# A perceiver kernel: the latents' own keys handled as one full 128-row tile, high and low part in one

## The reference

```
xn = _layernorm(x, ln1_w, ln1_b)            # the context, 1024 rows a batch
ln = _layernorm(latents, ln2_w, ln2_b)      # the 64 latents
q = ln @ Wq
kv = concatenate([xn, ln], axis=-2) @ Wkv   # 1024 context keys, then 64 own keys
k, v = split(kv, 2)                         # 16 heads of 64
logits = einsum('bhld,bhsd->bhls', q * scale, k * scale)
out = einsum('bhls,bhsd->bhld', softmax(logits), v)
return out.reshape(B, L, INNER) @ Wo
```

## Time and profile before

| | us |
|---|---|
| median of 3 runs (lowest, highest) | 920.51 (920.04, 922.19) |
| the profiled execution | 921.28 |
| its span, first to last instruction | 919.6 |
| PE busy | 812.8 |
| DVE busy | 530.1 |
| ACT busy | 385.0 |
| POOL busy | 256.7 |

### The profile page before, as it was taken

The page is one execution under the profiler, slowest core; times in us unless marked ns, Lnnn a source line. Parts: engine busy times, 40 slices in busy tenths (PEclk is TensorE's granted clock), DMA queues, the critical chain, the costliest instruction groups (busy, mean ns, idle before and its releaser), DMA issues.

```text
span 919.6 us, 13716 instructions
## 1 busy us (share of the span) xinstructions
PE 812.8 (88%) x5443; PEld 699.2 (76%) x5443; DVE 530.1 (58%) x992; ACT 385.0 (42%) x888; POOL 256.7 (28%) x179
## 2 busy tenths in 40 slices
PE   5899999999999999999999999997636565788996
PEld 3589999999999999999999999984312232257885
DVE  5364565555555555556547453445899999971112
ACT  2444444443544443444444343432853434403341
POOL 3717008008005205303502600001245545610000
PEclk9999999999999999999999999997858989898998
DMA  8100100100100010010030100000200000061720
GB/s 297 46 1 1 47 1 2 46 2 1 42 6 1 6 42 1 1 47 1 2 115 1 10 1 1 1 1 2 92 0 0 0 1 0 0 240 37 273 92 25
DMA packets 22499, 34.21 MB, mean 37 GB/s; under 512 B 6488, under 2 KB 18336, under 8 KB 21408
## 3 DMA queue, kind: packets, MB, share of 16 engines
q1 hardware_dynamic: 22432, 33.29, 10.6%
HBM read 32.77 MB, written 0.52 MB: 36 GB/s over the span
## 4 chain that ended last, share of the span: by engine, by line
PE 76%; DVE 16%; issue 4%; DMA 1%; ACT 1%; SPq 0%; DVEq 0%; POOL 0%; POOLq 0%; ACTq 0%
PE psum L1155 21%; PE psum L1193 20%; DVE state L782 12%; PE psum L1176 6%; PE psum L1197 4%; PE psum L1128 3%; PE psum L1475 3%; PE psum L1465 3%; PE psum L1216 2%; PE psum L1111 2%; PE psum L1135 2%; PE psum L1226 2%; PE psum L1207 2%; PE psum L1288 1%; DMA wq_sb<-in_L_xattn_Wq_dram 1%
## 5 line engine op out<-in xcount | busy, mean ns | idle before, releaser
L901 ACT ACTIVATE pt_hi<-psum 128x512 fp32r<-128x512 f32 (+1 forms) x192 | 87.0, 488 | 268.6 <-PE psum L1176 169.8
L624 DVE TENSOR_TENSOR pt_lo<-psum,pt_hi 128x512 fp32r<-128x512 f32 (+1 forms) x192 | 100.3, 550 | 101.4 <-ACT pt_hi L901 101.2
L1193 PE MATMUL psum<-kvn_hi,pt_hi 128*128 128x256 f32 x512 | 149.6, 292 | 0.0
L1193 PE MATMUL psum<-kvn_lo,pt_hi 128*128 128x256 f32 x512 | 144.0, 281 | 0.0
L1193 PE MATMUL psum<-kvn_hi,pt_lo 128*128 128x256 f32 x512 | 143.8, 281 | 0.0
L632 DVE TENSOR_REDUCE rowmax<-psum 128x1 f32<-128x728 f32 x64 | 58.7, 918 | 110.0 <-PE psum L1155 110.0
L782 DVE TENSOR_TENSOR_SCAN state<-dec,drive 128x2048 f32<-128x2048 f32 x16 | 107.1, 6691 | 0.1
L1193 PEld LDWEIGHTS psum<-kvn_lo,pt_hi 128*128 128x128 f32 x512 | 97.3, 190 | 0.1
L1193 PEld LDWEIGHTS psum<-kvn_hi,pt_hi 128*128 128x128 f32 x512 | 97.1, 190 | 0.1
L1193 PEld LDWEIGHTS psum<-kvn_hi,pt_lo 128*128 128x128 f32 x512 | 97.1, 190 | 0.0
L1155 PE MATMUL psum<-kvt_hi,qk_hi 128*128 128x364 f32 (+1 forms) x384 | 90.7, 345 | 4.3 <-ACT prob L939 2.5
(11 more groups left out here) (216 smaller groups left out, 1471.0 us busy)
## 6 DMA issues: line engine op xcount, KB each, us to landing
w<-in_L_ffn_W_dram SPq DMA_DIRECT2D x16, 1024.0 KB, 7.5
ctx_nat<-in_ctx_dram SPq DMA_DIRECT2D x8, 1024.0 KB, 4.9
wk_nat<-in_L_xattn_Wkv_dram SPq DMA_DIRECT2D x1, 1024.0 KB, 6.5
wq_sb<-in_L_xattn_Wq_dram SPq DMA_DIRECT2D x1, 1024.0 KB, 11.7
wv<-in_L_xattn_Wkv_dram SPq DMA_DIRECT2D x1, 1024.0 KB, 13.9
wo<-in_L_xattn_Wo_dram SPq DMA_DIRECT2D x1, 1024.0 KB, 16.2
q_t<-in_L_attn_W_in_dram SPq DMA_DIRECT2D x1, 1024.0 KB, 7.4
x_lat<-in_x_dram SPq DMA_DIRECT2D x1, 512.0 KB, 3.7
```

The source lines that it names most:

```text
L624: dve.tensor_tensor(pt_lo[u][rows, t0:t1, :], where[rows, 0:(t1 - t0) * P].rearrange("p (t m) -> p t m", m=P), pt_hi[u][rows, t0:t1, :].bi ...
L901: act.activation(pt_hi[u][rows, t0:t1, :], where[rows, 0:(t1 - t0) * P].rearrange("p (t m) -> p t m", m=P), ACT.Copy)\
L1193: pe.matmul(PV, w[u][:, j, :], x_[slot][:, j, :], start=(j == 0 and w is pt_hi and x_ is kvn_hi), stop=False)
```

## The change

The own keys are treated as a full tile of 128 rows. A third Exp writes the 64 own probabilities a second time behind the first (`prob` becomes 64 columns wider). One transpose of these 128 columns then gives the turned own probabilities twice, on the upper and the lower 64 partitions. ACT evacuates both into `pt_hi`; DVE then replaces the half `half(1)` (partitions 64 to 127) by the low part, value minus its high part. The latents are laid out on both halves as well: SP copies them by two DMAs inside the SBUF from `x_lat` to the two halves of `lat_cur`, and POOL makes `cur_hi` on all 128 partitions and `cur_lo` on the first 64, the rest staying zero. `cur_hi` and `cur_lo` have a buffer for each slot. The product with `cur_hi` then gives hi x hi + lo x hi in one matmul, the one with `cur_lo` hi x lo. The turn is the same in even and odd blocks.

```diff
@@ -77,8 +77,8 @@
         qk_lo = [sb(att, f"qk_lo{i}", [P, CK, HP, 2, L], F32R) for i in range(2)]
         x_lat = sb(att, "x_lat", [P, TT, C])
         lat_cur = sb(att, "lat_cur", [P, C])
-        cur_hi = sb(att, "cur_hi", [P, C], F32R)
-        cur_lo = sb(att, "cur_lo", [P, C], F32R)
+        cur_hi = [sb(att, f"cur_hi{i}", [P, C], F32R) for i in range(2)]
+        cur_lo = [sb(att, f"cur_lo{i}", [P, C], F32R) for i in range(2)]
         latt_hi = sb(att, "latt_hi", [P, CK, T], F32R)
         latt_lo = sb(att, "latt_lo", [P, CK, T], F32R)
 
@@ -86,7 +86,7 @@
         wk_t = sb(att, "wk_t", [P, HP, C])
         wv = sb(att, "wv", [P, CK, INNER])
         wo = sb(att, "wo", [P, HP, C])
-        prob = [sb(att, f"prob{i}", [P, S + L]) for i in range(2)]
+        prob = [sb(att, f"prob{i}", [P, S + 2 * L]) for i in range(2)]
         y_n = sb(att, "y_n", [P, C])
         y_t = sb(att, "y_t", [P, CK, P])
         o_t = sb(att, "o_t", [P, HP, P])
@@ -119,7 +119,7 @@
         kvn_hi[1] = sb(att, "kvn_hi1", [P, SJ, C], F32R)
         kvn_lo[1] = sb(att, "kvn_lo1", [P, SJ, C], F32R)
         pt_hi = [sb(att, f"pt_hi{i}", [P, SJ + 1, P], F32R) for i in range(2)]
-        pt_lo = [sb(att, f"pt_lo{i}", [P, SJ + 1, P], F32R) for i in range(2)]
+        pt_lo = [sb(att, f"pt_lo{i}", [P, SJ, P], F32R) for i in range(2)]
         att.close()
 
 
@@ -238,6 +238,7 @@
         TWO = psum[:, 0:2, :]
         CUT = 364
         LG_A, LG_B = psum[:, 0:2, 0:CUT], psum[:, 2, 0:S + L - 2 * CUT]
+        LG_OWN = psum[:, 2, S - 2 * CUT:S + L - 2 * CUT]
         TP, PV, OC, MB = [psum[:, 3, :], psum[:, 4, :]], psum[:, 5, 0:C], psum[:, 6, :], psum[:, 7, :]
 
         XB = (0, 1, 3, 6)
@@ -247,6 +248,7 @@
         ld_xlat, ld_vec, ld_wq, ld_wk, ld_wvo, ld_ctx = (sem(n) for n in (
             "ld_xlat", "ld_vec", "ld_wq", "ld_wk", "ld_wvo", "ld_ctx"))
         ld_vec2 = sem("ld_vec2")
+        ld_lat = sem("ld_lat")
         ld_mam, ld_idx, ld_comb, ld_b2, ld_out = (sem(n) for n in ("ld_mam", "ld_idx", "ld_comb", "ld_b2", "ld_out"))
         ld_e = [sem(f"ld_e{i}") for i in range(RING)]
 
@@ -351,11 +353,19 @@
             sp.dma_start(wo[:], Wo.rearrange("(h p) n -> p h n", p=P)).then_inc(ld_wvo, 16)
             sp.dma_start(x1[:], x.rearrange("(t b) l c -> (b l) t c", b=BP)).then_inc(ld_wvo, 16)
 
+            def load_latents(b):
+                for h in range(2):
+                    sp.dma_start(lat_cur[half(h)], x_lat[half(b % BP), b // BP, :]).then_inc(ld_lat, 16)
+
+            sp.wait_ge(s_pln, 1)
+            load_latents(0)
             for b in range(1, B):
                 sp.wait_ge(s_misc, MISC * b)
                 sp.wait_ge(s_klo, b)
                 sp.dma_start(ctx_nat[:], ctx_in[b].rearrange("(p j) c -> p j c", j=SJ))\
                     .then_inc(ld_ctx, 16)
+                sp.wait_ge(s_lcur, 2 * b)
+                load_latents(b)
 
             sp.wait_ge(s_qcur, 2 * B)
             sp.dma_start(win[:], W_in.rearrange("(k p) n -> p k n", p=P)).then_inc(ld_mam, 16)
@@ -421,6 +431,8 @@
 
             link(pool.memset(ident[:], 0.0))
             link(pool.memset(q_cur[:], 0.0))
+            for slot in range(2):
+                link(pool.memset(cur_lo[slot][half(1)].bitcast(F32), 0.0))
             pool.affine_select(out=ident[:], in_=ident[:], compare_op=ALU.not_equal, fill=1.0, base=0,
                                pattern=[[-1, P]], channel_multiplier=1).then_inc(s_id, 1)
             link(pool.memset(mhalf[:], -0.5))
@@ -436,7 +448,7 @@
 
                 pool.wait_ge(s_misc, MISC * (b - 1) + 4)
                 apart(pool)
-                pool.wait_ge(s_lcur, 3 * b)
+                pool.wait_ge(s_lcur, 2 * b)
                 apart(pool)
                 for h in range(2):
                     rows = slice(h * DH, (h + 1) * DH)
@@ -445,17 +457,14 @@
 
             def latents(b, slot):
 
-                rows = half(slot)
-                flat = x_lat[:].rearrange("p t c -> p (t c)")
+                top_rows = half(0)
                 pool.wait_ge(s_klo, b + 1)
                 apart(pool)
-                pool.tensor_copy(lat_cur[rows], flat[rows, ds((b - slot) * (C // BP), C)]).then_inc(s_lcur, 1)
-                pool.wait_ge(s_lcur, 3 * b + 1)
-                apart(pool)
-                pool.tensor_scalar(cur_hi[rows], lat_cur[rows], 1.0, 0.0, ALU.mult, ALU.add).then_inc(s_lcur, 1)
-                pool.wait_ge(s_lcur, 3 * b + 2)
-                pool.tensor_tensor(cur_lo[rows], lat_cur[rows], cur_hi[rows].bitcast(F32), ALU.subtract)\
-                    .then_inc(s_lcur, 1)
+                pool.wait_ge(ld_lat, 32 * (b + 1))
+                pool.tensor_scalar(cur_hi[slot][:], lat_cur[:], 1.0, 0.0, ALU.mult, ALU.add).then_inc(s_lcur, 1)
+                pool.wait_ge(s_lcur, 2 * b + 1)
+                pool.tensor_tensor(cur_lo[slot][top_rows], lat_cur[top_rows], cur_hi[slot][top_rows].bitcast(F32),
+                                   ALU.subtract).then_inc(s_lcur, 1)
 
             def context(b, slot):
 
@@ -498,7 +507,7 @@
                     queries(b + 1)
                     context(b + 1, 1 - slot)
                     latents(b + 1, 1 - slot)
-                    pool.wait_ge(s_lcur, 3 * (b + 2))
+                    pool.wait_ge(s_lcur, 2 * (b + 2))
 
             all_steps(body, lambda b, slot, pair: None)
 
@@ -620,10 +629,12 @@
                 high, low, where, t0, t1 = {"A": (s_hA, s_lA, TP[0], 0, 4), "B": (s_hB, s_lB, TP[1], 4, 8),
                                             "C": (s_hC, s_lC, TP[0], 8, 9)}[part]
                 dve.wait_ge(high, count(b, hp))
-                rows = slice(0, P) if part != "C" else half(slot)
-                dve.tensor_tensor(pt_lo[u][rows, t0:t1, :],
-                                  where[rows, 0:(t1 - t0) * P].rearrange("p (t m) -> p t m", m=P),
-                                  pt_hi[u][rows, t0:t1, :].bitcast(F32), ALU.subtract).then_inc(low, 1)
+                if part == "C":
+                    dve.tensor_tensor(pt_hi[u][half(1), SJ, :], where[half(1), 0:P],
+                                      pt_hi[u][half(1), SJ, :].bitcast(F32), ALU.subtract).then_inc(low, 1)
+                    return
+                dve.tensor_tensor(pt_lo[u][:, t0:t1, :], where.rearrange("p (t m) -> p t m", m=P),
+                                  pt_hi[u][:, t0:t1, :].bitcast(F32), ALU.subtract).then_inc(low, 1)
 
             def step(b, slot, hp, live, more, pair):
                 p1, p3 = back(b, slot, hp, 1), back(b, slot, hp, 3)
@@ -897,9 +908,8 @@
                 turned, high, where, t0, t1 = {"A": (s_tA, s_hA, TP[0], 0, 4), "B": (s_tB, s_hB, TP[1], 4, 8),
                                                "C": (s_tC, s_hC, TP[0], 8, 9)}[part]
                 act.wait_ge(turned, count(b, hp))
-                rows = slice(0, P) if part != "C" else half(slot)
-                act.activation(pt_hi[u][rows, t0:t1, :],
-                               where[rows, 0:(t1 - t0) * P].rearrange("p (t m) -> p t m", m=P), ACT.Copy)\
+                act.activation(pt_hi[u][:, t0:t1, :],
+                               where[:, 0:(t1 - t0) * P].rearrange("p (t m) -> p t m", m=P), ACT.Copy)\
                     .then_inc(high, 1)
 
             def mean_value(now):
@@ -936,8 +946,10 @@
                     act.activation(prob[hp % 2][:, 0:2 * CUT].rearrange("p (a n) -> p a n", n=CUT), LG_A, ACT.Exp,
                                    bias=nbias[slot][:, hp:hp + 1], scale=SCALE,
                                    accum_out=den_part[slot][:, hp, 0:1])
-                    act.activation(prob[hp % 2][:, 2 * CUT:], LG_B, ACT.Exp, bias=nbias[slot][:, hp:hp + 1],
-                                   scale=SCALE, accum_out=den_part[slot][:, hp, 1:2]).then_inc(s_exp, 1)
+                    act.activation(prob[hp % 2][:, 2 * CUT:S + L], LG_B, ACT.Exp, bias=nbias[slot][:, hp:hp + 1],
+                                   scale=SCALE, accum_out=den_part[slot][:, hp, 1:2])
+                    act.activation(prob[hp % 2][:, S + L:], LG_OWN, ACT.Exp, bias=nbias[slot][:, hp:hp + 1],
+                                   scale=SCALE).then_inc(s_exp, 1)
                 if more and hp == MISC - 1:
                     misc_hi(b + 1, 1 - slot, hp)
                     own_rows(b + 1, 1 - slot)
@@ -1161,11 +1173,7 @@
                 if part == "C":
                     pe.wait_ge(s_lA, count(b, hp))
                     apart(pe)
-                    if slot == 0:
-                        last = pe.transpose(TP[0][0:L, 0:P], prob[hp % 2][:, S:S + L], ident[:])
-                    else:
-                        last = pe.matmul(TP[0][half(slot), 0:P], prob[hp % 2][:, S:S + L], ident[:],
-                                         start=True, stop=True)
+                    last = pe.transpose(TP[0][:, 0:P], prob[hp % 2][:, S:S + 2 * L], ident[:])
                     last.then_inc(s_tC, 1)
                     return
                 before = back(b, slot, hp, 1)
@@ -1183,7 +1191,7 @@
```

(7 more changed lines are left out.)

## The result

| | before | after |
|---|---|---|
| median, us | 920.35 | 892.92 |
| lowest to highest | 920.04 to 922.19 | 892.84 to 893.45 |
| the profiled execution (span) | 921.28 (919.6) | 892.84 (891.1) |
| first logits to the end of the stage's last L1226 / L1233 | 39.58 to 627.90: 588.3 | 39.09 to 601.87: 562.8 |
| behind the attention stage | 291.7 | 289.3 |

The ratio is 0.9699, with a 95% interval of 0.9682 to 0.9716: 27.4 us faster. The forecast was 894.5.

A forecast was written before the change was run, and what follows sets the result against it. TensorE was taken as the bound. Gains of 25.7 us in steps and 0.7 in the drain, less 0.2 for the Exp, gave 26.2 off 921.28, stated as 894.5 us for the median; range 890 to 904.

The forecast's parts named there:

- The bound and the way to read it: Attention stage: TensorE has no idle time to fill, so only giving it less work gains; costs read from ends.
- Parts 1 and 2: Own products and turn: one product (0.12) and shape changes into (0.19) and out of 64 rows (0.13) go; turn 0.11.
- Part 3: Head's output behind a full-width transpose at step end: 0.38 us, taken as already carrying a shape entry.
- The first rival: At the head's output the shape change is only moved: step gains 0.22 to 0.30, about 904 us; chance 0.14.
- The sum: Attention stage: 25.7 us from the steps plus 0.7 in the drain, 26.4; less 0.2 for the Exp, 26.2.
- Part 4: ScalarE's third Exp: signal 0.12 to 0.23 later, hidden behind TensorE, cover left 0.3 to 0.4; 0.2 charged at start.
- two covers at the ends of steps: Last step of a block: 0.95 us before the next block's logits, and over 2 us for the Exp itself.
- Parts 6 and 7: GpSimd loses one copy (0.39) and SP gains two on-chip copies per block, both under cover: nothing charged.

The follow-up runs named there:

- the run with equal work: Changed kernel with its second own product (cur_lo) on the upper 64 rows only, as many matmuls as before that edit: 914.25 us.
- two-product variant: Kernel before the change with its third own product (low probabilities times high latents) left out, two 64-row products staying: 911.89 us.

## Why the prediction was right

- *The bound and the way to read it.* Right: before the change TensorE had no idle time from the third step to the drain, and less work for it went into the time almost one for one.
- *Parts 1 and 2, product, two changes of shape, turn.* Right in each term. The product is 0.12 by the run without it (a step of 8.53 against 8.65) and about 0.10 by the run with one more (6.5 us in the stage); the shape is 0.34 at its place and 0.32 in the mean of all steps by the run with equal work, against 0.32 from the earlier trace rows.
- *Part 3, 0.38 for the head's output behind a full turn.* Right: 0.38 in both parities and in the drain. I had taken it from the earlier trace rows, the one place where L1216 stood behind a certain change. The first rival (902 to 907) fails. L1216 took 0.38 behind L1165, though both are shown 128*64, and the trace of the kernel before has a border there. Behind the transpose L1165 the loads for L1216 start 0.23 later, together with their matmul:

```profile
234.54 0.11 PEld L1165 LDWEIGHTS psum<-ident,prob 128*64 128x64 f32 x1
234.77 0.31 PEld L1216 LDWEIGHTS psum<-y_t,wv 128*64 128x64 f32 x8
```

  Behind L1167 of odd blocks, a plain matmul in the same shape, L1216 starts 0.01 later. This is explained if L1165 worked as a full-array instruction. It fits what the Trainium skill says in "TensorEngine Tiling (Array Packing)", "Restrictions", on transposes and column tiling; no run separates it from another cause. The drain that the Trainium skill names in the same page's "Key Properties" agrees with the loads that start late at every border looked at here.
- *The sum.* Forecast 26.2 in the attention stage, measured 25.5. Odd blocks gave 0.40 to 0.43 a step but for hp = 3. Even blocks gave 12.4 in 30 steps where I had 12.9: most steps 0.41 to 0.46, but hp = 5 and 6 only 0.39, as their 24 products of the context take 0.03 more (last end less first, 2.73 against 2.70), and hp = 3 of block 0 only 0.25. I didn't find the cause of the 0.03; in eight steps it is worth 0.3 us. The drain gave about 1.3 (24.58 to 23.28, from the last logits on) where I had 1.1 with the last step. The stage thus gave 0.7 less than forecast, and what lies outside it gave some 2 us that I had put at nothing. That the two make 892.9 beside a forecast of 894.5 is in part luck.
- *Part 4, the third Exp.* Right that it is hidden, and its cover was called right (0.3 to 0.4, measured 0.35). Its size was low: the next activation starts 0.20 later, not 0.12, as ScalarE's timeline at the end of block 1 shows, answering to the earlier trace rows:

```profile
170.67 0.31 ACT L951 ACTIVATE prob<-psum,nbias 128x64 f32<-128x64 f32 x1
170.87 0.60 ACT L890 ACTIVATE kvt_hi<-psum 128x512 fp32r<-128x512 f32 x1
...
171.51 0.69 DVE L594 TENSOR_TENSOR kvt_lo<-psum,kvt_hi 128x512 fp32r<-128x512 f32 x1 [0.48 <-ACT kvt_hi L890]
...
172.55 0.76 PE L1167 MATMUL psum<-kvt_hi,qk_hi 128*128 128x364 f32 x3
```

  At the start of the stage this is paid, as I had said of the earlier trace rows, 0.22 and 0.12 us, 0.34 in all where I had charged 0.24:

```profile
45.96 0.91 PE L1167 MATMUL psum<-kvt_hi,qk_hi 128*128 128x364 f32 x3 [2.74 <-ACT prob L951]
```

- *What I missed.* I named two covers at the ends of steps and not the third: y_t on VectorE, behind the context's scaling in hp = 3. When TensorE became 0.4 faster there, y_t became the later one and kept 0.16 of it in three steps and 0.23 in hp = 3 of block 0: 0.7 us.
- *Parts 6 and 7.* Right: GpSimd's cur_hi waits for its own kvn_lo alone. An on-chip copy lands about 5 us after its issue, as the DMA view shows, most of a block ahead of its use; seven of the eight pairs are issued 0.4 us behind a context load of 1024 KB, so the 5 us are not those of a copy alone:

```profile
lat_cur<-x_lat SPq DMA_DIRECT2D x16, 64.0 KB, 5.0
```

- *The rest of the 27.4.* Behind the attention stage the profiled execution is 2.4 us shorter, though nothing there was changed; I had allowed 1 or 2. One place is the projection after the stage, in the chain of waits before and after (start, us, what):

```profile
635.32 9.98 PE psum L1288 x16
```

```profile
609.27 8.99 PE psum L1295 x16
```

  The same sixteen matmuls, both times at half pace at first (0.85 us from end to end, then 0.43), before for two more of them than after: 1.0 us. Another is the end of the kernel, where before, and not after, TensorE stood idle once more ahead of its last two turns, 1.2 us longer in all from the last L1451 (L1458):

```profile
916.40 0.59 PE L1497 MATMUL psum<-ident,acc_t 128*128 128x128 f32 x2 [1.53 <-issue]
```

  Over the nine kernels profiled the part behind the stage lasted 288.5 to 291.7 us, and the kernel before had the longest of them, while its two-product variant had 289.5. So I take 25.5 for the effect of the change, and the 2.4 us for differences between executions, part of it the clock and part the idle time at the end. That last is inferred from the spread; no run set it apart.

## What to carry to other kernels

Read a matmul's price from the distance between neighbours' ends, and look first where the array's shape changes in TensorE's view: leaving out rows or columns there can cost more than streaming zeros through the full array. Both pieces of work tried here, each alone in its shape once a step, were faster widened to the full shape, by computing something twice or filling it with a part that is needed anyway, than cut down to their size; how many pieces of one small shape in a row would turn this around, no run here shows. When TensorE is the bound and gets faster, list every signal that it waits for in each kind of step, with its spare time: the y_t that was missed here was the one with the least.

## What was not expected of the hardware

- A product on half the rows, alone among full ones, costs more than the full one: 0.31 us to its end and 0.26 to the next instruction's, where the full one has 0.12 and 0.11.
- Four full passes of 128 columns, half of whose results are not used, beat eight passes of 64 columns, 0.88 against 0.96 us with the turns behind them.
- Behind a 128x64 Exp from PSUM the next activation starts 0.20 us after it, behind a Copy of the same shape 0.12. The Exp takes its bias from a 128x1 operand in the SBUF, the Copy has none; the Trainium skill's page "ScalarE: Activation LUTs", section "What ACT_TABLE_LOAD costs", puts about 93 ns on such an operand, and the 0.08 between the two agrees.
